# One encoder layer on one core: first key stack issued by ScalarE, and another order of steps on every engine

## The reference

```python
Q, K, V = (split_heads(x @ W.T + b) for W, b in ((Wq, bq), (Wk, bk), (Wv, bv)))
scores = Q @ K.T / sqrt(8)
scores = where(causal_mask, -inf, scores) - delta          # delta = i - j
x = layernorm(x + (softmax(scores) @ V).merge_heads() @ Wo.T + bo)
h = silu(x @ w1.T * s1) * (x @ w2.T * s2)                  # 128 -> 512
h = gelu(h @ h1.T * sh1)                                   # 512 -> 512
h = gelu(h @ h2.T * sh2)                                   # 512 -> 512
out = layernorm(x + h @ w3.T * s3)                         # 512 -> 128
```

## Time and profile before

| | us |
|---|---|
| median of 3 runs (lowest, highest) | 792.68 (790.08, 795.04) |
| profiled execution, its own time | 793.55 |
| its span, first to last instruction | 791.8 |
| PE, DVE busy in the span | 732.7, 634.9 |
| ACT, POOL busy in the span | 551.3, 509.0 |

### The profile page before, as it was taken

One profiled execution on the slowest core, in us unless ns is written; L12 is line 12 of the kernel. 1 busy time (PEld: TensorE's weight loads), 2 busy tenths in 40 slices (PEclk: granted clock), 3 DMA queues, 4 the chain that ended last, 5 costly groups with the idle time before them and its releaser, 6 DMA issues.

```text
span 791.8 us, 18746 instructions
## 1 busy us (share of the span) xinstructions
PE 732.7 (93%) x6026; PEld 500.2 (63%) x6026; DVE 634.9 (80%) x2759; ACT 551.3 (70%) x874; POOL 509.0 (64%) x616
## 2 busy tenths in 40 slices
...
PEclk9557669999999999999999999999999999999998
...
GB/s 220 151 31 45 44 89 23 121 19 75 81 18 138 16 131 26 125 17 92 62 33 123 17 136 20 126 29 95 46 52 104 16 140 17 113 29 27 17 1 28
DMA packets 36778, 53.28 MB, mean 67 GB/s; under 512 B 5288, under 2 KB 16872, under 8 KB 36680
## 3 DMA queue, kind: packets, MB, share of 16 engines
...
## 4 chain that ended last, share of the span: by engine, by line
PE 52%; DVE 32%; issue 8%; POOL 3%; ACT 3%; DMA 1%; SPq 1%; DVEq 0%; POOLq 0%; ACTq 0%
DVE ps L946 19%; PE ps L576 10%; PE ps L681 9%; PE ps L582 8%; DVE m L946 6%; PE ps L662 5%; PE ps L595 4%; DVE den L986 4%; PE ps L664 4%; PE ps L621 2%; PE ps L602 2%; PE ps L747 2%; PE ps L739 2%; PE ps L637 1%; PE ps L696 1%
## 5 line engine op out<-in xcount | busy, mean ns | idle before, releaser
L946 DVE CUSTOM_DVE_ANT_0 ps<-ps,causal 128x256 f32<-128x256 f32 (+1 forms) x928 | 296.5, 390 | 15.1 <-PE ps L624 13.0
L797 ACT ACTIVATE pt<-ps 128x768 f32<-128x768 f32 x256 | 196.0, 816 | 37.5 <-PE ps L664 33.7
L1093 POOL TENSOR_SCALAR_AFFINE_SELECT pt<-pt 128x512 f32<-128x512 f32 x256 | 161.1, 640 | 90.2 <-ACT pt L797 87.0
L1139 POOL TENSOR_TENSOR hlo<-hf,hhi 128x512 fp32r<-128x512 f32 x128 | 162.0, 1287 | 60.1 <-ACT hhi L880 59.9
L870 ACT ACTIVATE hf<-ps,vec_sb 128x512 f32<-128x512 f32 x128 | 88.0, 688 | 115.5 <-PE ps L582 113.7
L576 PE MATMUL ps<-hhi,h_hi 128*128 128x512 f32 x496 | 148.4, 420 | 1.9 <-ACT hhi L819 1.6
L582 PE MATMUL ps<-hlo,h_hi 128*128 128x512 f32 x496 | 137.8, 399 | 1.0 <-POOL hlo L1139 0.8
L946 DVE DVE_READ_ACCUMULATOR2_ANT m<- 128x1 f32 x928 | 128.2, 138 | 0.0
L582 PEld LDWEIGHTS ps<-hlo,h_hi 128*128 128x128 f32 x496 | 94.0, 190 | 26.1 <-POOL hlo L1139 4.2
L681 PE MATMUL ps<-pt,vst 128*32 128x256 f32 (+1 forms) x2048 | 107.1, 339 | 1.2 <-POOL pt L1093 1.0
L576 PEld LDWEIGHTS ps<-hhi,h_hi 128*128 128x128 f32 x496 | 84.6, 189 | 24.5 <-issue 3.2
...
## 6 DMA issues: line engine op xcount, KB each, us to landing
...
den<-raw SPq DMA_DIRECT2D x64, 64.0 KB, 2.0
num<-raw SPq DMA_DIRECT2D x64, 64.0 KB, 2.0
...
```

Source lines behind the costliest of these rows:

```text
L797: nc.scalar.activation(pt[u][:, c:c + 2, :], ps[:, first:last + 1, 0:3 * P], ACT.Exp).then_inc(t_free.sem, 1)
L946: part = nc.vector.tensor_tensor_reduce(ps[:, bank, cols], ps[:, bank, cols], mask, 1.0, LOWEST, ALU.add, ALU.max, m32[b][:, it, c + e, u: ...
L1093: nc.gpsimd.affine_select(out=diag, in_=diag, compare_op=ALU.is_ge, fill=0.0, base=0, pattern=[[0, 2], [0, 2], [1, P]], channel_multiplier ...
L1139: nc.gpsimd.tensor_tensor(h_lo[layer % 2][:, m, :], hf[:, n % 4, :], h_hi[layer % 2][:, m, :].bitcast(F32), ALU.subtract).then_inc(hlo_rea ...
```

## The change

`kstack` for pair 0 leaves SP's list and becomes a step of ScalarE, which issues its six DMAs on ScalarE's own queue after `qhi 1 0`. On DVE `qlo 1 0` (the low part of the key) goes ahead of `vadd 0`. All lists of all engines have a new order. In the fill the second head group of a sequence comes in another mix of `s`, `s1` and `st`, `arec 0 0` comes three `smax1` sooner, and SP loads the second half of the weights (`wload 1`) behind `qstack 1`. The number of steps is the same, but that slots begin and end elsewhere in the flow (`hhi 1 3`, `gelu 2 0` and one `repack` and `tload` pass from one list's start to the other's end).

```diff
@@ act
+                    elif kind == "kstack":
+                        b = s[1]
+                        act.wait_ge(rows_done, ROWS_DONE)
+                        qklo_ready.wait(act, 0, 2)
+                        cols = slice(b * T, b * T + T)
+                        for part, letter in enumerate(K_PARTS):
+                            src = (qk_hi if letter == "h" else qk_lo)[1]
+                            nc.scalar.dma_start(ks[0][part::4, :, cols].bitcast(F32),
+                                                src[:, cols].bitcast(F32)).then_inc(half_stacked[b], 16)
 ACT_FILL = [
-    ("qhi", 0, 0), ("rows", 0), ("qhi", 1, 0), ("qhi", 0, 1), ("w_hi", 0), ("qhi", 1, 1), ("w_hi", 1),
+    ("qhi", 0, 0), ("rows", 0), ("qhi", 1, 0), ("kstack", 0, 0), ("kstack", 1, 0), ("w_hi", 0), ("qhi", 0, 1),
+    ("qhi", 1, 1), ("w_hi", 1), ("exp", 0, 0, 0), ("exp", 0, 1, 0), ("exp", 0, 2, 0), ("exp", 0, 3, 0),
 DVE_FILL = [
-    ("rows", 0), ("qlo", 0, 0), ("vadd", 0), ("qlo", 1, 0), ("smax1", 1, 0, 0, 0), ("smax", 0, 0, 0),
+    ("rows", 0), ("qlo", 0, 0), ("qlo", 1, 0), ("vadd", 0), ("smax", 0, 0, 0), ("smax", 0, 1, 0),
...
 SP_FILL = [
-    ("tload", 0), ("xload", 1), ("wload", 0), ("qstack", 0, 0), ("kstack", 0, 0), ("kstack", 1, 0),
-    ("qstack", 1, 0), ("wload", 1), ("qstack", 1), ("kstack", 1), ("mTd", 0, 0, 0), ("mTd", 0, 1, 0),
+    ("xload", 1), ("wload", 0), ("qstack", 0, 0), ("qstack", 1, 0), ("qstack", 1), ("wload", 1), ("kstack", 1),
+    ("mTd", 0, 0, 0), ("mTd", 0, 1, 0), ("tload", 0), ("mTd", 1, 0, 0), ("mTd", 1, 1, 0),
...
 PE_ORDER = [
-    ("s", 0, 3, 0), ("s", 0, 4, 0), ("h", 1, 1, -2), ("s", 0, 5, 0), ("h", 1, 2, -2), ("s", 0, 6, 0),
-    ("s", 0, 7, 0), ("h", 1, 3, -2), ("wo", -1), ("s", 1, 0, 0), ("s", 1, 1, 0), ("h", 2, 0, -2), ("mT", 0, 0),
-    ("h", 2, 1, -2), ("s", 1, 2, 0), ("s", 1, 3, 0), ("h", 2, 2, -2), ("s", 1, 4, 0), ("x1t", -1),
-    ("s", 1, 5, 0), ("h", 2, 3, -2), ("s", 1, 6, 0), ("s", 1, 7, 0), ("qq", 1), ("g", 0, -1), ("w3h", -2),
-    ("u", 0, -1), ("st", 0, 0, 0), ("st", 0, 1, 0), ("qk", 1), ("w3l", -2), ("st", 0, 2, 0), ("st", 0, 3, 0),
-    ("u", 1, -1), ("g", 1, -1), ("mT", 1, 0), ("st", 0, 4, 0), ("st", 0, 5, 0), ("pv", 0, 0, 0), ("g", 2, -1),
-    ("st", 0, 6, 0), ("st", 0, 7, 0), ("zt", 2, -2), ("pv", 0, 1, 0), ("st", 1, 0, 0), ("u", 2, -1),
-    ("g", 3, -1), ("st", 1, 1, 0), ("st", 1, 2, 0), ("pv", 0, 2, 0), ("pv", 0, 3, 0), ("st", 1, 3, 0),
+    ("s", 0, 3, 0), ("s", 0, 4, 0), ("h", 1, 1, -2), ("h", 1, 2, -2), ("s", 0, 5, 0), ("s", 0, 6, 0),
+    ("h", 1, 3, -2), ("s", 0, 7, 0), ("wo", -1), ("s", 1, 0, 0), ("h", 2, 0, -2), ("mT", 0, 0), ("s", 1, 1, 0),
+    ("s", 1, 2, 0), ("h", 2, 1, -2), ("s", 1, 3, 0), ("h", 2, 2, -2), ("s", 1, 4, 0), ("s", 1, 5, 0),
+    ("x1t", -1), ("h", 2, 3, -2), ("s", 1, 6, 0), ("s", 1, 7, 0), ("qq", 1), ("g", 0, -1), ("u", 0, -1),
+    ("w3h", -2), ("st", 0, 0, 0), ("st", 0, 1, 0), ("qk", 1), ("w3l", -2), ("st", 0, 2, 0), ("st", 0, 3, 0),
+    ("g", 1, -1), ("mT", 1, 0), ("st", 0, 4, 0), ("st", 0, 5, 0), ("pv", 0, 0, 0), ("u", 1, -1), ("g", 2, -1),
+    ("st", 0, 6, 0), ("st", 0, 7, 0), ("zt", 2, -2), ("pv", 0, 1, 0), ("st", 1, 0, 0), ("g", 3, -1),
+    ("u", 2, -1), ("st", 1, 1, 0), ("st", 1, 2, 0), ("pv", 0, 2, 0), ("pv", 0, 3, 0), ("st", 1, 3, 0),
 ACT_ORDER = [
-    ("hhi", 1, 3, -2), ("gelu", 2, 0, -2), ("gelu", 2, 1, -2), ("lnnorm", 1, -1), ("hhi", 2, 0, -2),
-    ("gelu", 2, 2, -2), ("x1hi", -1), ("x1c", -1), ("hhi", 2, 1, -2), ("hhi", 2, 2, -2), ("gelu", 2, 3, -2),
-    ("hhi", 2, 3, -2), ("qhi", 0, 1), ("tanh", 0, -1), ("exp", 0, 0, 0), ("exp", 0, 1, 0), ("qhi", 1, 1),
+    ("lnnorm", 1, -1), ("hhi", 2, 0, -2), ("gelu", 2, 1, -2), ("hhi", 2, 1, -2), ("x1hi", -1), ("x1c", -1),
+    ("gelu", 2, 2, -2), ("gelu", 2, 3, -2), ("hhi", 2, 2, -2), ("hhi", 2, 3, -2), ("qhi", 0, 1),
+    ("tanh", 0, -1), ("exp", 0, 0, 0), ("exp", 0, 1, 0), ("qhi", 1, 1), ("exp", 0, 2, 0), ("exp", 0, 3, 0),
...
 DVE_ORDER = [
-    ("smax", 0, 3, 0), ("smax", 0, 4, 0), ("smax", 0, 5, 0), ("arec", 1, -1), ("smax", 0, 6, 0),
+    ("smax", 0, 3, 0), ("smax", 0, 4, 0), ("arec", 1, -1), ("smax", 0, 5, 0), ("smax", 0, 6, 0),
-    ("mTl", 0, 0), ("smax", 1, 2, 0), ("smax", 1, 3, 0), ("smax", 1, 4, 0), ("smax", 1, 5, 0), ("x1lo", -1),
+    ("smax", 1, 2, 0), ("smax", 1, 3, 0), ("mTl", 0, 0), ("smax", 1, 4, 0), ("smax", 1, 5, 0), ("x1lo", -1),
 POOL_ORDER = [
-    ("glo", 3, -2), ("xbo", -1), ("amul", 0, -1), ("hlo", 1, 0, -2), ("amul", 1, -1), ("hlo", 1, 1, -2),
-    ("hlo", 1, 2, -2), ("hlo", 1, 3, -2), ("rstd", 1, -1), ("hlo", 2, 0, -2), ("hlo", 2, 1, -2),
+    ("glo", 3, -2), ("amul", 0, -1), ("hlo", 1, 0, -2), ("hlo", 1, 1, -2), ("amul", 1, -1), ("hlo", 1, 2, -2),
+    ("xbo", -1), ("hlo", 1, 3, -2), ("rstd", 1, -1), ("hlo", 2, 0, -2), ("hlo", 2, 1, -2), ("hlo", 2, 2, -2),
 SP_ORDER = [
-    ("repack", 0, 0, 0, -1), ("repack", 0, 0, 1, -1), ("repack", 1, 1, 0, -1), ("repack", 1, 1, 1, -1),
-    ("repack", 1, 0, 0, -1), ("repack", 1, 0, 1, -1), ("mTd", 0, 0, 0), ("mTd", 0, 1, 0), ("tload", 0),
+    ("repack", 0, 1, 1, -1), ("tload", -1), ("repack", 0, 0, 0, -1), ("repack", 0, 0, 1, -1),
+    ("repack", 1, 1, 0, -1), ("repack", 1, 1, 1, -1), ("repack", 1, 0, 0, -1), ("repack", 1, 0, 1, -1),
 DVE_DRAIN = [
-    ("arec", 0, -1), ("gmul", 3, -2), ("arec", 1, -1), ("res1", -1), ("lnstat", 1, -1), ("x1lo", -1),
+    ("gmul", 3, -2), ("arec", 0, -1), ("arec", 1, -1), ("res1", -1), ("lnstat", 1, -1), ("x1lo", -1),
```

More of the change, by code:

```diff
@@ L90 @@
-    ("exp", 0, 1, 1), ("table", "exp", -1), ("exp", 0, 2, 1), ("exp", 0, 3, 1), ("exp", 0, 4, 1),
-    ("exp", 0, 5, 1), ("lnnorm", 1, 0), ("x1hi", 0), ("x1c", 0), ("tanh", 0, 0), ("qhi", 0, 2),
-    ("exp", 0, 6, 1), ("tanh", 1, 0), ("qhi", 1, 2), ("ghi", 0, 0), ("exp", 0, 7, 1), ("tanh", 2, 0),
-    ("exp", 1, 0, 1), ("exp", 1, 1, 1), ("tanh", 3, 0), ("exp", 1, 2, 1), ("exp", 1, 3, 1), ("exp", 1, 4, 1),
-    ("ghi", 1, 0), ("exp", 1, 5, 1), ("exp", 1, 6, 1), ("ghi", 2, 0), ("exp", 1, 7, 1), ("ghi", 3, 0),
@@ L95 @@
-    ("araw", 1, 1), ("gelu", 1, 0, 0), ("hhi", 1, 0, 0), ("gelu", 1, 1, 0), ("gelu", 1, 2, 0), ("hhi", 1, 1, 0),
-    ("hhi", 1, 2, 0), ("gelu", 1, 3, 0), ("table", "gelu", 1),
+    ("qhi", 0, 0), ("rows", 0), ("qhi", 1, 0), ("kstack", 0, 0), ("kstack", 1, 0), ("w_hi", 0), ("qhi", 0, 1),
+    ("qhi", 1, 1), ("w_hi", 1), ("exp", 0, 0, 0), ("exp", 0, 1, 0), ("exp", 0, 2, 0), ("exp", 0, 3, 0),
+    ("exp", 0, 4, 0), ("exp", 0, 5, 0), ("exp", 0, 6, 0), ("exp", 0, 7, 0), ("exp", 1, 0, 0), ("exp", 1, 1, 0),
@@ new lines @@
+    ("exp", 1, 2, 0), ("exp", 1, 3, 0), ("exp", 1, 4, 0), ("exp", 1, 5, 0), ("exp", 1, 6, 0), ("exp", 1, 7, 0),
+    ("araw", 1, 0), ("exp", 0, 0, 1), ("exp", 0, 1, 1), ("exp", 0, 2, 1), ("exp", 0, 3, 1), ("lnnorm", 1, 0),
+    ("x1hi", 0), ("x1c", 0), ("exp", 0, 4, 1), ("exp", 0, 5, 1), ("table", "exp", -1), ("tanh", 0, 0),
+    ("qhi", 0, 2), ("qhi", 1, 2), ("tanh", 1, 0), ("exp", 0, 6, 1), ("ghi", 0, 0), ("tanh", 2, 0),
+    ("ghi", 1, 0), ("exp", 0, 7, 1), ("exp", 1, 0, 1), ("exp", 1, 1, 1), ("tanh", 3, 0), ("exp", 1, 2, 1),
@@ L97 @@
+    ("exp", 1, 3, 1), ("exp", 1, 4, 1), ("exp", 1, 5, 1), ("ghi", 2, 0), ("exp", 1, 6, 1), ("exp", 1, 7, 1),
+    ("ghi", 3, 0), ("araw", 1, 1), ("table", "gelu", 1), ("gelu", 1, 0, 0), ("hhi", 1, 0, 0), ("gelu", 1, 1, 0),
+    ("hhi", 1, 1, 0), ("gelu", 1, 2, 0), ("hhi", 1, 2, 0), ("gelu", 1, 3, 0), ("hhi", 1, 3, 0),
+    ("gelu", 2, 0, 0),
 ]
 DVE_FILL = [
-    ("rows", 0), ("qlo", 0, 0), ("vadd", 0), ("qlo", 1, 0), ("smax1", 1, 0, 0, 0), ("smax", 0, 0, 0),
-    ("smax", 0, 1, 0), ("smax1", 1, 0, 1, 0), ("smax", 0, 2, 0), ("smax", 0, 3, 0), ("smax", 0, 4, 0),
```

71 lines of the change are left out of this document (34 added, 37 removed), and 63 rows, old and new, of tables (DVE_FILL, PE_DRAIN, PE_FILL).

## The result

The changed kernel takes 789.34 us (median of 20 runs) against 791.28 for the one before (20 runs): a ratio of 0.9968, with an interval from 0.9954 to 0.9982, so 1.4 to 3.6 us faster. The forecast was 0.9 slower: 789.34 lies inside its range of 785 to 801.5, but the time moved the other way, by less than 0.5%. The profiled execution took 787.43 (span 785.6).

A forecast was written before the change was run, and what follows sets the result against it. Slots bound it, one half by DVE, the other by PE. Slots +7.0, start -1.8, rest of fill -1.0, drain -3.3 sum to +0.9 on the profiled 793.55, 794.5; less 0.87 to the median, forecast 793.6, range 785 to 801.5.

The forecast's parts named there:

- PE's half: Slot from `qq` to `s 0 0`: `u 1` behind `pv 0 0` loses its cover, +0.47; `g 2` no longer waits, -0.1.
- ACT's chain: In each slot, two `hhi` instead of one ahead of `qhi 0` make exponentials 0 to 0.3 later; taken as +0.1.
- DVE's half: Slot from first `smax` to `x1lo`, chain almost wholly on DVE; gain claimed there is the 0.17 of idle DVE.
- The 0.17: DVE's one idle time in its half of a slot, before `smax 1 2`, claimed to go with the change.
- the two edits to which I put it down: In DVE's half: `s 1 2` issued ahead of `h 2 1`, `mTl` no longer before it; claimed gain 0.17 a slot.
- Sum of the slots: PE's half and ACT's chain together: some +0.5 a slot, +7.0 in fourteen slots, bounds -2.4 and +14.
- The start: First scores at 19.9, 2.2 sooner, through ScalarE's queue; 0.4 given back, so -1.8, bounds +0.4 and -2.3.
- The rest of the fill: Fill after the first scores: `arec 0` three `smax1` sooner, one more `st` left behind; -1.0, bounds +3 and -4.
- the named unknown, the clock: PE's lower or upper clock in the fill; ten us of PE work at one or the other make five.
- The drain: After the slots: `gmul 3` ahead of `arec 0` and a shorter late PE stop; -3.3, bounds -2.1 and -4.0.
- POOL's second stop: In the drain, PE's later stop at 748.41 for POOL shrinks by 0.7 to 1.4, as the second `amul` comes sooner.

The follow-up runs named there:

- the run with SP's stacks: The changed kernel with the first pair's k stacks issued by SP again, between q's two halves; 789.89 us, ratio to before 0.9978.

## Why the prediction was wrong

- *PE's half: right in mechanism, too large.* `pv 0 0` is pinned and `u 1` loses its cover. Up to `st 0 6` it costs 0.38, where I had 0.47 - 0.1; between `pv 0 1` and `st 1 0` 0.1 of that is given back, which I had put at nothing. So the move costs 0.27 to 0.28, 1.3 less in all.
- *ACT's chain: +0.1 was +0.0.* I counted the second `hhi` in full ahead of `qhi 0`, and left out that `gelu 2 3` starts as much sooner when it no longer stands behind the first. The swap leaves ACT's total the same.
- *DVE's half: the step that failed.* The term for it in the slot's sum was nothing. The 0.17 was used up against ACT's delay and never subtracted from the slot, though the text itself said that DVE sets the time there. It is -0.14, 2.0 in all, the largest miss of the three. And the two edits to which I put it down lose 0.55 when made alone: not only waits changed, since PE needs 0.37 more for a pair pulled apart. PE's, DVE's and POOL's orders of this half together give the gain; smaller parts lost, but not every part was tried.
- *Sum of the slots:* +0.28 - 0.14 = +0.14 instead of +0.5, thus +2.0 in fourteen slots instead of +7.0 (0.4 of the difference is the rounding of 0.47 to 0.5). This made the sign: with +2.0 the same sum is -4.1.
- *The start: the first scores came 1.6, 1.6 and 0.9 sooner* (20.48, 20.53 and 21.22 in three executions, against 22.09) where 2.2 was forecast (19.9): they began 3.0 behind the last issue (17.51), and I had taken 2.0. How much of it reaches the slots the timings leave between 0 and 1.6; I had counted on 1.8, and nothing as late behind it. That `wload 1` had to move for it, I did not see: with ScalarE's queue and `wload 1` left in its place, the first scores came at 23.95, against 22.09 before and 21.19 with `wload 1` moved. The Trainium skill, "DMA: Bandwidth & Descriptors", section "Issuing engines are not separate DMA queues", says that DMAs started by several engines interleave on the same 16 DMA engines. The trace agrees: with the issues of both and the weights, these were 1.03 busy from 16 to 22.
- *The rest of the fill: -1.0 with a bound of -4;* start and fill together were -3.0 (-4.3 to -1.7) against -2.8 forecast. That the sum fits is in part luck, as the start gave less than its share and the rest more, and the reason was half seen: half of it is the first `qq` (-1.6), half the named unknown, the clock (-1.5), and that not where the clock rises but where it falls again, in the first slot. Each us at the lower level cost 0.35 there, not the half that I reckoned with. Which moves bring the first `qq` sooner was not tried.
- *The drain: -3.3 was -2.2.* The swap of `gmul 3` alone gave 2.4, where 2.1 to 2.4 was forecast. The 0.7 to 1.4 for POOL's second stop did not come: that stop of 0.65 (still 0.62 with the swap alone) shrank to 0.17, but PE then waited 0.54 for ACT's `lnnorm` ahead of `x1t` (746.65).
- *By the measured parts,* +2.0 - 3.0 - 2.2 is -3.2; by their ratios the two timings of the change gave -2.5 (-3.6 to -1.4) and -4.6 (-6.2 to -3.1).

Which edit of the fill keeps the clock up for longer was not tried part by part; ScalarE's queue is not needed for it, since the run with SP's stacks had 1.00 there in its profile. Why the same program has the fall in some executions and not in others stays open.
